# Three passes of a fused kernel hand their weights, halves and first rows on to the pass ahead

## The chip, the cores and the metric

The kernel runs on one core of a Trainium2 chip. The metric is device time in microseconds (us); three runs of the kernel before gave 2746.31, 2747.47 and 2748.63, the median is 2747.47. The profile is of one execution, with a span of 2744.8 us from the first to the last instruction.

## The reference

Two layers over x (8 batches of 512 rows of 512 values). Each adds a gated attention and a gated feed-forward to x, each after a layer norm:

```python
x = x + tanh(g_xattn[0]) * L0_xattn(layernorm(x), fside, fside, ctx, Wq, Wk, Wv, Wlq, Wlk, Wo, bo)
x = x + tanh(g_ffn[0])   * L0_ffn(layernorm(x), w1, conv_w, conv_b, w2)      # ternary weights, depthwise conv, silu
x = x + tanh(g_xattn[1]) * L1_xattn(layernorm(x), ctx, ctx, Wq, bq, Wk, bk, Wv, bv, Wo, bo)
x = x + tanh(g_ffn[1])   * L1_ffn(layernorm(x), wf, uf, bf, wi, ui, bi, wc, uc, bc, wo, uo, bo, in_c)
```

The first attention has 16 heads over 512 keys with a router matrix between queries and keys; the third line attends to 77 context rows. The last line is a recurrence over the 8 batches: `f, i = sigmoid(x wx + c wu + b)`, `g = tanh(...)`, `c = f * c + i * g`, and an output projection with the last state.

## The kernel before

Six passes run one after the other: context, attention, feed-forward, context attention, recurrence, output. A `Pass` has its own SBUF tiles, PSUM banks and semaphores; between two passes all engines meet at a barrier and the semaphores are cleared. Each pass writes its rows to a scratch tensor in HBM (`heads`, `x2`, `x3`, `columns`), and the next reads them.

In a pass each engine runs a hand-written list of instructions with semaphore waits, in the same order each turn; a turn is one batch of 512 rows. `clock` runs turn 0, a hardware loop over the middle turns, and the last two turns written out. Engines take their instructions in order: a wait holds all that stands behind it on that engine. SyncE issues nearly all DMAs, also in order.

A matrix product in full precision is made of three products of halves: a tile is split into a high half (ScalarE's copy to float32r) and a low half (VectorE's subtraction of the high half from the tile). `Weights` (line 120) does this for a pass's weights at its start: `load` on SyncE, `hi` on ScalarE, `lo` on VectorE, and TensorE waits for the last low half. `LayerNorm` (line 456 on) takes statistics and aggregates on VectorE (`moments`), a power on GpSimd (`pool_power`), and scales on VectorE (`scale`).

What stands at the starts:

- Feed-forward (`quantised_ffn_pass`): SyncE loads the output weights `Wo` of the attention (L133), the first heads (L1116) and first rows (L1117), then small constants, among them the convolution weights (L1124) and 16 loads of the convolution's bias `cb` (L1128). TensorE's `attention_out` (L1197 to L1202) needs the halves of the weights and of the heads and the bias row `BO` (L1348, L1462). VectorE waits for all constants, makes the diagonals (L1465, L1467), and adds the rows (`row_tile`, L1485).
- Context attention (`context_attention_pass`): SyncE loads three small constants (L1763 to L1765), the first rows, `Wq` and `Wo`, then keys and values. ScalarE first waits for the constants and takes a tanh (L1930), then makes high halves. VectorE makes low halves, then normalises the first rows. TensorE transposes them (L1863) and projects them to queries (L108).
- Recurrence (`recurrence_pass`): rows first, then eight loads in stages: three input weights `WX`, three state weights `WU` (each stage is free again once its low half is made), and the output's two at the end. TensorE transposes rows (L2176), then multiplies them with `WX` (L2186) and, after two column groups, the first state with `WU` (L2201).

What stands in the tails: in the attention, turn 7, quad 3 is the last quad of heads; ScalarE takes exponentials (L901), GpSimd sums them (L726, L730), and the sums gate the last output. In the feed-forward, the last turn has no next batch; VectorE scales hidden pairs (L1530, `scaled`), takes maxima of magnitudes (L1538, `magnitude`, then `fold`), TensorE convolves (L1243, waits for `scaled`), and after `fold` the token maxima, the quantisation and the second product of the last batch follow one after the other. In the context attention a turn has four groups; in each VectorE takes maximum and difference of the scores (L2011, L2014), ScalarE exponentials (L1959) and copies (L1954), GpSimd the probabilities (L1837) and, in the fourth group, the residual (L1842). TensorE's scores of the next group (L1887) wait for VectorE's difference of the present one.

## Time and profile before

| | us |
|---|---|
| median of three runs | 2747.47 |
| the profiled execution | 2746.55 |
| its span, first to last instruction | 2744.8 |

| engine | busy us | share of the span |
|---|---|---|
| TensorE, matmuls | 2364.8 | 86% |
| VectorE | 1412.0 | 51% |
| ScalarE | 1027.8 | 37% |
| GpSimd | 599.5 | 22% |

| pass | from | to | TensorE busy | VectorE busy | ScalarE busy |
|---|---|---|---|---|---|
| context | 0 | 115 | 73.3 | 53.5 | 41.6 |
| attention | 115 | 1063 | 838.3 | 488.4 | 414.6 |
| feed-forward | 1063 | 1636 | 478.2 | 379.6 | 269.4 |
| context attention | 1636 | 2055 | 344.4 | 287.3 | 169.9 |
| recurrence (to the first output loads) | 2055 | 2640 | 539.0 | 166.9 | 116.9 |
| output | 2640 | 2745 | 91.7 | 36.4 | 15.4 |

A row of the timeline gives the start and the length of an instruction or a merged run of the same one, its engine, line, operation, output and inputs, and the count; in brackets stands how long the engine sat idle ahead of it and what ended that. SPq is SyncE's queue of DMA issues: its length is the time of issuing, not that of the transfer. Idle time counts only where the engine is the one that others wait for.

### The profile page before, as it was taken

What the parts mean: (1) busy time and instruction counts of PE and PEld (TensorE: products, weight loads), DVE (VectorE), ACT (ScalarE), POOL (GpSimd) and SP (SyncE); (2) the same over time, 40 slices, a digit from 0 to 9 for tenths busy, and PEclk for the clock granted to TensorE, in tenths of its full rate; (3) what the DMA queues carried; (4) which work ended last, traced back from release to release, by engine and by line L of the source; (5) the groups of instructions that cost most, each with busy time, mean ns of one, the idle gap of its engine ahead of it and who ended that gap; (6) DMA issues with size and microseconds to landing.
All of it is one profiled execution on the core that took longest, in us unless ns stands there. A gap on an engine that the chain in (4) does not pass through costs nothing. (4 is left out here: it accounts for less than half of the span.)

```text
span 2744.8 us, 40758 instructions
## 1 busy us (share of the span) xinstructions
PE 2364.8 (86%) x16307; PEld 1555.8 (57%) x16348; DVE 1412.0 (51%) x1733; ACT 1027.8 (37%) x1185; POOL 599.5 (22%) x204
## 2 busy tenths in 40 slices
PE   7259999999999994789999866998977999999978
PEld 6235545555555552444454424666755788888856
DVE  5345555554555542577677646887734222222224
ACT  3324453444544542444555533444433111111211
POOL 0004554553645553000000001333220000000000
PEclk9669999999999997899999987999987999999989
DMA  7701011010110004011111011222114111111156
GB/s 237 179 33 37 15 42 44 10 45 10 45 41 14 13 9 134 33 43 51 46 55 53 17 68 66 70 82 69 68 58 164 47 46 46 46 46 46 46 230 259
DMA packets 104571, 182.56 MB, mean 67 GB/s; under 512 B 17252, under 2 KB 39780, under 8 KB 99358
## 3 DMA queue, kind: packets, MB, share of 16 engines
q1 hardware_dynamic: 100110, 172.84, 19.0%
q10 hardware_dynamic: 4368, 8.39, 0.8%
q8 instruction: 69, 1.13, 0.2%
q14 instruction: 24, 0.20, 0.0%
HBM read 122.07 MB, written 59.15 MB: 66 GB/s over the span
## 5 line engine op out<-in xcount | busy, mean ns | idle before, releaser
L973 DVE TENSOR_REDUCE att_mx<-att_sn 128x2 f32<-128x1024 f32 x256 | 313.7, 1225 | 189.9 <-PE att_sn L818 187.2
L730 POOL TENSOR_TENSOR att_es<-att_es,att_num 128x2048 f32<-128x2048 f32 x64 | 292.7, 4574 | 15.7 <-ACT att_num L901 9.4
L901 ACT ACTIVATE att_num<-att_st 128x2048 f32<-128x2048 f32 x128 | 240.4, 1878 | 131.0 <-PE att_st L806 67.0
L726 POOL TENSOR_TENSOR att_es<-att_num 128x2048 f32<-128x2048 f32 x32 | 145.8, 4558 | 395.8 <-PE att_pj L788 379.2
L2287 ACT ACTIVATE rec_ga<-rec_g,rec_bg 128x512 f32<-128x512 f32 x84 | 57.2, 689 | 311.9 <-PE rec_g L2186 311.9
L818 PE MATMUL att_sn<-att_kh,att_qh 32*128 32x512 f32 x512 | 128.7, 498 | 26.3 <-DVE att_mx L973 26.3
L1530 DVE TENSOR_TENSOR ffn_hs<-ffn_h,ffn_fb 128x1024 f32<-128x1024 f32 x64 | 78.1, 1220 | 115.9 <-PE ffn_h L1230 106.9
L1230 PE MATMUL ffn_h<-ffn_xqt,ffn_w 128*128 128x512 bf16 x486 | 118.8, 388 | 16.7 <-DVE ffn_hs L1530 13.1
L818 PEld LDWEIGHTS att_sn<-att_kh,att_qh 32*128 32x128 f32 x512 | 48.9, 188 | 146.1 <-DVE att_mx L973 100.0
L1837 POOL TENSOR_TENSOR xat_pr<-xat_e,xat_rd 128x1232 f32<-128x1232 f32 x32 | 73.1, 2284 | 244.0 <-DVE xat_rd L2023 237.2
L781 PE MATMUL att_pj<-att_num,att_v 128*32 128x512 f32 x1024 | 123.5, 602 | 1.0 <-issue 1.0
L1243 PE MATMUL ffn_c<-ffn_hs,ffn_dg 32*32 32x512 f32 x3072 | 114.2, 629 | 10.7 <-issue 4.2
L476 POOL TENSOR_TENSOR ffn_ln_rstd<-ffn_ln_var,ffn_ln_power 128x4 f32<-128x4 f32 x8 | 18.4, 2297 | 440.8 <-DVE ffn_ln_var L497 440.8
L2355 DVE SCALAR_TENSOR_TENSOR rec_ga<-rec_ga,rec_c 128x512 f32<-128x512 f32 x32 | 22.1, 690 | 171.4 <-ACT rec_ga L2287 171.4
L1382 ACT ACTIVATE ffn_ss<-ffn_c,ffn_cb 128x512 f32<-128x512 f32 x128 | 77.4, 692 | 70.7 <-PE ffn_c L1243 65.3
L476 POOL TENSOR_TENSOR rec_ln_rstd<-rec_ln_var,rec_ln_power 128x4 f32<-128x4 f32 x8 | 8.5, 1059 | 432.6 <-DVE rec_ln_var L497 432.6
L1954 ACT ACTIVATE xat_pt<-xat_pt 77x512 f32<-77x512 f32 x128 | 73.7, 588 | 77.7 <-PE xat_pt L1896 77.3
L1230 PEld LDWEIGHTS ffn_h<-ffn_xqt,ffn_w 128*128 128x128 bf16 x512 | 47.6, 100 | 86.3 <-issue 21.9
L1278 PE MATMUL ffn_a<-ffn_w,ffn_sq 128*128 128x512 bf16 x338 | 81.8, 387 | 11.0 <-ACT ffn_sq L1404 9.4
L1896 PEld LDWEIGHTS xat_pt<-xat_ident,xat_pr 128*77 128x77 f32 x512 | 62.8, 152 | 45.4 <-issue 23.3
L1896 PE MATMUL xat_pt<-xat_ident,xat_pr 128*77 128x128 f32 x512 | 78.6, 285 | 9.4 <-POOL xat_pr L1837 7.9
L1404 ACT ACTIVATE ffn_sq<-ffn_s 128x2048 bf16<-128x2048 int8 x32 | 61.3, 1916 | 66.1 <-DVE ffn_s L1565 66.1
(375 smaller groups left out, 5873.3 us busy)
## 6 DMA issues: line engine op xcount, KB each, us to landing
att_x<-in_x SPq DMA_DIRECT2D x8, 1024.0 KB, 5.5
att_f<-in_fside_BxSxS SPq DMA_DIRECT2D x8, 1024.0 KB, 7.6
heads<-att_o SPq DMA_DIRECT2D x32, 256.0 KB
ffn_ol<-heads SPq DMA_DIRECT2D x8, 1024.0 KB, 5.3
ffn_x<-in_x SPq DMA_DIRECT2D x8, 1024.0 KB, 5.5
x<-ffn_xr SPq DMA_DIRECT2D x32, 256.0 KB, 2.0
xat_x<-x SPq DMA_DIRECT2D x8, 1024.0 KB, 5.2
xat_xr<-x SPq DMA_DIRECT2D x8, 1024.0 KB
```

Source lines behind the costliest of these rows:

```text
L726: pool.tensor_tensor(ES[:], E[0][:], E[1][:], ALU.add).then_inc(s_sum, 1)
L730: pool.tensor_tensor(ES[:], ES[:], E[k][:], ALU.add).then_inc(s_sum, 1)
L781: last = pe.matmul(out[heads(j), :], V[:, k, c * P + DH * j:c * P + DH * j + DH], E[k][:, j, :], start=(k == 0), stop=(k == T - 1))
L818: last = pe.matmul(sn_ps[:, r, :], QT[0][c][own, m // 2 * P:m // 2 * P + P], KT[0][c][own, :], start=True, stop=True)
L901: act.activation(E[k][:], st_ps[:], ACT.Exp, scale=SCALE).then_inc(s_exp, 1)
L973: dve.tensor_reduce(MX[c % 2][:, m // 2, 2 * DH * (m % 2):2 * DH * (m % 2) + DH + 1:DH], sn_ps[:], AX, ALU.max, negate=True).then_inc(s_ma ...
L1230: last = pe.matmul(h_ps[:, m, :], W1[:, k, i * P:i * P + P], XQT[:, k, :], start=(k == 0), stop=(k == C - 1))
L1243: last = pe.matmul(c_ps[quarter(m), r, :], DG[quarter(r), 3 * (HG * group + m) + k, :], HS[group % 2][quarter(r), m, k:k + S], start=(k == ...
L1278: last = pe.matmul((a_ps, b_ps)[OUT_BANK[front][t]][:], SQ[:, i, t * P:t * P + P], W2[:, i, :], start=(i == 0), stop=(i == HT - 1))
L1382: act.activation(SS[:, i, :], c_ps[:, r, :], ACT.Silu, bias=CB[:, i:i + 1]).then_inc(s_silu, 1)
L1530: dve.tensor_tensor(HS[group % 2][:, 2 * half:2 * half + 2, 1:S + 1], h_ps[:], FB[:].unsqueeze(1).broadcast_to([P, 2, S]), ALU.mult).then_ ...
L1896: last = pe.transpose(pt_ps[j % 2][0:G, t * P:t * P + P], PR[d % 2][:, j, t, :], ident[:])
```

## The change

Tiles that were a pass's own become shared: `rows` and `rows_b` (rows and normalised rows), `weights_a` and `weights_b` (two pairs of halves), and three pairs `row_weights`. The weights that a pass needed at its start are loaded and split in the last turns of the pass ahead, and the first rows are loaded there too, for the context attention and the recurrence also normalised.

- Attention: SyncE, in its last turn, loads the feed-forward's `Wo`, the first rows and the first heads. Ahead of the last quad ScalarE makes two high halves (weights, heads) and VectorE two low halves (`following`).
- Feed-forward: its start has none of the three large loads and no halves. In its last turn SyncE loads `Wq` and `Wo` of the context attention; ScalarE makes both high halves after the third activation group (`next_high`), VectorE both low halves between hidden pairs 6 and 7 (`next_low`); then SyncE loads the first rows of `x2`, and VectorE normalises them ahead of the last maximum of magnitudes (`next_rows`).
- Context attention: ScalarE issues the loads of the three input weights into a new tile `STAGE` at the ends of groups (6,0), (6,2) and (7,0), and makes the high halves at the ends of (6,1), (6,3) and (7,1); VectorE makes the low halves there. SyncE loads the first rows of `x3`; VectorE takes their statistics at the end of group (7,2) and scales them at the end of (7,3), after a power on GpSimd.
- Recurrence: starts with three state weights to load; the two last output loads change places and stages.

```diff
@@ attention_pass
+            sp.wait_ge(made["x"], QUADS)
+            sp.wait_ge(made["f"], QUADS)
+            sp.dma_start(F[:], kxn(next_w)).then_inc(s_nextw, 16)
+            sp.dma_start(X[:], rows(x, 0)).then_inc(s_nextx, 16)
+            sp.wait_ge(made["k"], QUADS)
+            sp.wait_ge(s_store, C * 16)
+            sp.dma_start(f32(W_QO[1][1][:]), rows(o_s, 0)).then_inc(s_nexto, 16)
             turn(B - 1)
...
+            def following():
+
+                act.wait_ge(s_nextw, 16)
+                act.wait_ge(made["q"], QUADS)
+                act.activation(W_QO[0][0][:], F[:], ACT.Copy).then_inc(s_nexthi, 1)
+                act.wait_ge(s_nexto, 16)
+                act.wait_ge(made["k"], QUADS)
+                act.activation(W_QO[1][0][:], f32(W_QO[1][1][:]), ACT.Copy).then_inc(s_nexthi, 1)
...
+            def following():
+
+                dve.wait_ge(s_nexthi, 1)
+                dve.tensor_tensor(W_QO[0][1][:], F[:], f32(W_QO[0][0][:]), ALU.subtract).then_inc(s_nextlo, 1)
+                dve.wait_ge(s_nexthi, 2)
+                dve.tensor_tensor(W_QO[1][1][:], f32(W_QO[1][1][:]), f32(W_QO[1][0][:]),
+                                  ALU.subtract).then_inc(s_nextlo, 1)
...
@@ quantised_ffn_pass
-            w.load(sp)
-            sp.dma_start(f32(OL[:]), batch_rows(o_s, 0)).then_inc(s_o, 16)
-            sp.dma_start(X[:], batch_rows(x, 0)).then_inc(s_x, 16)
+            sp.sem_inc(s_o, 16)
+            sp.sem_inc(s_x, 16)
             sp.dma_start(undo[:], undo_s).then_inc(s_undo, 16)
...
+            sp.wait_ge(s_rows, B * ROWS_N)
+            sp.dma_start(XN[:], kxn(next_wq)).then_inc(s_nextw[0], 16)
+            sp.wait_ge(s_xm, B)
+            sp.dma_start(X[:], kxn(next_wo)).then_inc(s_nextw[1], 16)
+            sp.wait_ge(s_nextlo, 2)
+            sp.wait_ge(s_store, T * 16)
+            sp.dma_start(X[:], batch_rows(x2_s, 0)).then_inc(s_nextx, 16)
             turn(B - 1, True, False, False)
...
                 silu(b, 2)
+                if not front:
+                    next_high()
...
                 scaled(b, 6)
                 if front:
                     row_maxima(rows)
+                else:
+                    next_low()
                 scaled(b, 7)
...
                 if front:
                     scaled(b + 1, 0)
+                if not front:
+                    next_rows()
                 magnitude(b, 3)
                 fold(b)
...
@@ context_attention_pass
-            load_x(0)
-            w.load(sp)
+            sp.sem_inc(s_x, 16)
+            load_x(1)
             load_keys(0, 0)
...
+                if c == 3 and isinstance(b, int) and b == B - 1:
+                    ln.pool_power(pool, B)
...
+            def next_load(n):
+                if n:
+                    act.wait_ge(s_nextlo, n)
+                act.dma_start(STAGE[:], kxn(next_w[n])).then_inc(s_nextw, 16)
...
+            def next_low(n):
+
+                dve.wait_ge(s_nexthi, n + 1)
+                dve.tensor_tensor(NEXT[n][1][:], STAGE[:], f32(NEXT[n][0][:]), ALU.subtract).then_inc(s_nextlo, 1)
...
+                at = (b - B + 2) * C + c if isinstance(b, int) else -1
+                if 0 <= at < 6 and at % 2:
+                    next_low(at // 2)
+                if isinstance(b, int) and b == B - 1:
+                    if c == 2:
+                        dve.wait_ge(s_nextx, 16)
+                        ln.moments(dve, Steps(s_next, 0, ln.DVE_N))
+                    if c == 3:
+                        after = Steps(s_next, 0, ln.DVE_N)
+                        after.done = 2 * T + 1
+                        dve.wait_ge(made["x"], B * C)
+                        ln.scale(dve, B, after)
...
@@ recurrence_pass
-        names = [(gates[n][0], WX[n], 1.0) for n in range(3)] + \
-                [(gates[n][1], WU[n], 0.5) for n in range(3)] + [(wo, WO, 1.0), (uo, WX[0], 0.5)]
-        NW, NG = len(names), 6
-        whole_stages = [GA[:, 0:C, :], C2[:], X[:], XN[:]]
+        names = [(gates[n][1], WU[n], 0.5) for n in range(3)] + [(wo, WO, 1.0), (uo, WX[0], 0.5)]
+        NW, NG = len(names), 3
+        whole_stages = [GA[:, 0:C, :], C2[:], XN[:], SW[:]]
...
-            sp.dma_start(X[:], rows(x3_s, 0)).then_inc(s_x, 16)
+            sp.sem_inc(s_x, 16)
             load(sp, 0)
             load(sp, 1)
```

## Rows read from the trace of the kernel before

**Rows 1.** Timeline at the start of the feed-forward: start, length, engine, line, operation.

```profile
1068.59 1.91 ACT L138 ACTIVATE ffn_woh<-ffn_xn 128x2048 fp32r<-128x2048 f32 x1 [11.76 <-DMA ffn_xn<-in_L_xattn_Wo]
1070.53 2.29 DVE L143 TENSOR_TENSOR ffn_wol<-ffn_xn,ffn_woh 128x2048 fp32r<-128x2048 f32 x1 [10.88 <-ACT ffn_woh L138]
...
1076.48 0.77 PE L1197 MATMUL ffn_a<-ffn_bo,ffn_pick 128*128 128x512 f32 x1 [17.57 <-DVE ffn_bo L1462]
...
1083.60 0.39 DVE L1465 TENSOR_REDUCE ffn_diagonal<-ffn_ident 128x32 f32<-128x128 f32 x1 [7.38 <-DMA ffn_cb<-in_L_ffn_conv_b]
...
1085.70 0.74 DVE L1485 SCALAR_TENSOR_TENSOR ffn_x<-ffn_a,ffn_tgx,ffn_x 128x512 f32<-128x512 f32 x1
```

**Rows 2.** Timeline at the start of the context attention.

```profile
1640.82 0.20 ACT L1930 ACTIVATE xat_tg<-xat_tg 128x2 f32<-128x2 f32 x1 [19.97 <-DMA xat_bq<-in_L_xattn_bq]
...
1661.82 1.94 PE L1863 MATMUL xat_pj<-xat_ident,xat_xn 128*128 128x128 f32 x8 [29.51 <-DVE xat_xn L502]
...
1667.80 0.77 PE L108 MATMUL xat_pj<-xat_xth,xat_wqh 128*128 128x512 f32 x1 [1.50 <-DVE xat_xtl L2005]
```

**Rows 3.** Timeline at the start of the recurrence.

```profile
2055.65 0.09 POOL L2159 MEMSET rec_ones<- 2x2 f32 x1
...
2060.54 2.47 DVE L488 BATCH_NORM_STATS2 rec_ln_stats<-rec_x 128x6 f32<-128x512 f32 x4 [10.78 <-DMA rec_x<-x]
...
2063.72 1.02 POOL L476 TENSOR_TENSOR rec_ln_rstd<-rec_ln_var,rec_ln_power 128x4 f32<-128x4 f32 x1 [7.93 <-DVE rec_ln_var L497]
...
2066.84 1.94 PE L2176 MATMUL rec_pj<-rec_ident,rec_xn 128*128 128x128 f32 x8 [17.93 <-DVE rec_xn L502]
...
2075.19 0.79 PE L2186 MATMUL rec_g<-rec_xth,rec_wx0h 128*128 128x512 f32 x1 [1.41 <-DVE rec_xtl L2319]
```

**Rows 4.** Bias loads `cb`, by tile: count, shortest, median, longest ns; first and last start.

```profile
L1128 SPq DMA_DIRECT2D ffn_cb<-in_L_ffn_conv_b x16: 432/432/7212, 1067.6 to 1081.5; - x16
```

**Rows 5.** Timeline: a convolution of the feed-forward that follows on idle time.

```profile
1565.37 4.87 PE L1243 MATMUL ffn_c<-ffn_hs,ffn_dg 32*32 32x512 f32 x96 [2.90 <-ACT ffn_ss L1382]
```

**Rows 6.** Windows of TensorE: stretch, us, busy (x), granted clock, DMA share, GB/s.

```profile
1566.00:1567.00 1.00, 1.00 (x37) 0.50 0.08 16
```

**Rows 7.** Timeline of the feed-forward's last turn.

```profile
1588.60 1.22 DVE L1530 TENSOR_TENSOR ffn_hs<-ffn_h,ffn_fb 128x1024 f32<-128x1024 f32 x1 [3.67 <-PE ffn_h L1230]
...
1591.95 3.40 PE L1243 MATMUL ffn_c<-ffn_hs,ffn_dg 32*32 32x512 f32 x96
...
1599.79 2.29 DVE L1538 TENSOR_TENSOR ffn_am<-ffn_am,ffn_ab 128x2048 f32<-128x2048 f32 x1
```

**Rows 8.** Timeline of the attention's last quad.

```profile
1028.96 9.25 POOL L730 TENSOR_TENSOR att_es<-att_es,att_num 128x2048 f32<-128x2048 f32 x2
...
1032.28 1.88 ACT L901 ACTIVATE att_num<-att_st 128x2048 f32<-128x2048 f32 x1 [2.37 <-PE att_pj L781]
...
1040.24 4.54 POOL L726 TENSOR_TENSOR att_es<-att_num 128x2048 f32<-128x2048 f32 x1 [2.03 <-PE att_pj L788]
```

**Rows 9.** Timeline: VectorE's scaling in the context attention while GpSimd is busy.

```profile
1941.60 8.09 DVE L502 TENSOR_SCALAR xat_xn<-xat_x,xat_ln_mv,xat_ln_rstd 128x512 f32<-128x512 f32 x4
```

**Rows 10.** Timeline of the last two turns of the context attention.

```profile
1971.22 0.59 ACT L1954 ACTIVATE xat_pt<-xat_pt 77x512 f32<-77x512 f32 x1 [2.63 <-PE xat_pt L1896]
...
1977.58 1.13 PE L1887 MATMUL xat_s<-xat_k,xat_qt 32*128 32x77 f32 x32
...
1987.51 1.44 DVE L2011 TENSOR_REDUCE xat_mx<-xat_s 128x16 f32<-128x1232 f32 x1 [0.57 <-PE xat_s L1887]
...
1991.01 1.06 ACT L1954 ACTIVATE xat_pt<-xat_pt 77x512 f32<-77x512 f32 x2
...
1996.95 1.13 PE L1887 MATMUL xat_s<-xat_k,xat_qt 32*128 32x77 f32 x32
...
2027.74 4.52 POOL L1842 TENSOR_TENSOR xat_xr<-xat_xr,xat_bo 128x2048 f32<-128x2048 f32 x1
...
2034.21 0.69 DVE L2005 TENSOR_TENSOR xat_atl<-xat_pj,xat_ath 128x512 fp32r<-128x512 f32 x1 [8.76 <-ACT xat_ath L1949]
```

More of the change, by code:

```diff
@@ L638, in heads, with clock @@
             return slice(DH * j, DH * j + DH)
-        def clock(eng, step, ahead, late):
+        def clock(eng, step, ahead, late, following=None):
             ahead()
@@ L649, in clock @@
                 for i in range(C):
+                    if turn == B - 1 and i == C - 1 and following:
+                        following()
                     step(turn, i)
@@ L929, in late @@
                     job(task)
-            clock(act, step, ahead, late)
+            def following():
[5 more added lines that the diff above has]
+                act.activation(W_QO[1][0][:], f32(W_QO[1][1][:]), ACT.Copy).then_inc(s_nexthi, 1)
+            clock(act, step, ahead, late, following)
         @block.vector
@@ L1026, in late @@
                     job(task)
-            clock(dve, step, ahead, late)
+            def following():
[4 more added lines that the diff above has]
+                                  ALU.subtract).then_inc(s_nextlo, 1)
+            clock(dve, step, ahead, late, following)
 def row_broadcast(pe, out, columns, ident):
@@ L1101, in quantised_ffn_pass @@
         FIRST, LAST = 2, B - 2
+        s_nextw = [ps.sem(f"nextw{i}") for i in range(2)]
+        s_nexthi, s_nextlo, s_nextx, s_next = (ps.sem(n) for n in ("nexthi", "nextlo", "nextx", "next"))
         block = ps.block()
@@ L1181, in _ @@
             pe.wait_ge(s_ident, 11)
-            w.wait(pe)
             pe.wait_ge(s_bo2, 2)
@@ L1727, in context_attention_pass @@
         s_pt, s_pte = ps.sem("pt"), ps.sem("pte")
+        STAGE = ps.sb("stage", [P, C, D])
+        s_nextw = ps.sem("nextw")
+        s_nexthi, s_nextlo, s_nextx, s_next = (ps.sem(n) for n in ("nexthi", "nextlo", "nextx", "next"))
         block = ps.block()
@@ L1851, in _ @@
             pe.wait_ge(s_ident, 2)
-            w.wait(pe)
             def job(turn, task):
@@ L2291, in gates_and_state @@
                     state_high(act, b + 1, c)
-            for i in range(3, NG):
+            for i in range(NG):
                 high_half(act, i)
@@ L2311, in _ @@
         def _(dve):
-            first = Steps(s_dve, 0, ln.DVE_N)
-            dve.wait_ge(s_x, 16)
-            ln.rows(dve, 0, first)
+            dve.sem_inc(s_dve, ln.DVE_N)
+            dve.sem_inc(ln.s_var, 1)
             def rows_low(a):
@@ L2326, in _ @@
             dve.scalar_tensor_tensor(CC[:, :, 1], C0[:], 2.0, f32(CC[:, :, 0]), ALU.mult, ALU.subtract).then_inc(s_cc, 1)
-            for i in range(2, NG):
+            for i in range(NG):
                 low_half(dve, i)
```

132 lines of the change are left out of this document (72 added, 60 removed).

## The prediction

> **What bounds the kernel now.** I read the profile in this order: the engine shares of the page, the timeline around each start of a pass, the list of waits there, and the timeline of each pass's last turns. TensorE is busy 86% of the span, and most of what is missing lies where one pass hands over to the next. At the start of the feed-forward it waits 17.57 us for the first matmul [rows 1], at that of the context attention 29.51 us [rows 2], at that of the recurrence 17.93 us [rows 3]. Nothing else runs there: each stretch is a load, a split into halves and a normalisation, one after the other, so what shortens that chain shortens the run. The last turns, where the change puts this work, are the opposite: TensorE, ScalarE and VectorE hand tiles around with little slack, and each takes its instructions in order. So the sum is made per pass: what its start gives, less what the tail ahead of it costs.
>
> **Start of the feed-forward: -7.0.** The loads of the output weights, of the first heads and of the first rows leave SyncE's queue. The end of this start isn't the weights but the constants: VectorE waits until 1083.60 for the last of the 16 small bias loads and adds the first rows at 1085.70 [rows 1]. Of those 16, all but one issue in 0.43 us; one took 7.21 [rows 4]. That one is the first behind the three 1 MB loads, which I take to hold it. Gone, they give 7.21 - 0.43 = 6.8, and SyncE reaches the small loads some 0.8 earlier (three issues of about 0.5 less the wait for GpSimd's identity). The load of the convolution weights stays ahead of them and may hold the first for about 1. I take 7.0, bounds 6.3 and 7.6. TensorE's first products move from 1076.48 to about 1068.6, but their rows are added only at 1085.70 - 7.0, so TensorE idles for about 3 us in between. After an idle time of 2.90 us the 96 convolution matmuls took 4.87 us [rows 5] where 3.40 is usual [rows 7]: the granted clock shows 0.50, the lower level of 1.2 GHz, just behind the wait [rows 6]. So +1.5 (0 to 1.9).
>
> **Tail of the attention: +2.6.** Ahead of the last quad ScalarE makes two copies of 1.91 and VectorE two subtractions of 2.29 [rows 1]. ScalarE is free from about 1029.9, so its first exponential goes from 1032.28 to 1033.8, and the 1.5 shrinks to about 1.0 by GpSimd's first sum at 1040.24 [rows 8]. VectorE is idle there, but GpSimd runs two sums over 9.25 us [rows 8]. Does it hold VectorE? In the context attention four VectorE instructions that take 1.9 elsewhere took 8.09 beside GpSimd's [rows 9]. If the two exclude each other here, the second subtraction (after 2.29 for the first and the end of GpSimd's 1038.2) ends at about 1042.8, and the sum starts there: +2.6. With nothing held it is +1.0. I take 2.6, the nearest row, and 4 as the upper end.
>
> The Trainium skill says the same of the port (SBUF — State Buffer, SBUF: two separate sides): a VectorE instruction with two inputs in SBUF and a GpSimd instruction that reads SBUF lock each other out for a whole instruction. By it the term is 2.6 and by a free port 1.0; the row agrees, though of another instruction kind.
>
> **Start of the context attention: -22.0.** First rows come normalised and the weights split, so TensorE can transpose at once (about 1637). What is late next is the small constants: ScalarE waits for them until 1640.82 [rows 2], and its copy of the first columns stands behind. From the first transposition (1661.82) to the first projection (1667.80) it is 5.98, and the first 1.1 of it is done by then: 1641.0 + 4.9 = 1645.9, which is 21.9 earlier. Bounds 21.5 and 22.5. The next rows are loaded at once and hidden.
>
> **Tail of the feed-forward: +11.6.** VectorE takes its two low halves between its products for hidden pairs 6 and 7; the latter stands at 1588.60 [rows 7]. It waits for ScalarE, which makes the high half only after the third activation group, from about 1588.1 to 1590.0. Then two times 2.29: pair 7 starts at 1594.6, 6.0 late. TensorE's last convolution, at 1591.95, needs it: it starts at 1595.85, +3.9, and after that idle time at the low clock, +1.5 as above. The first rows of the next pass (statistics, power, scaling) stand ahead of VectorE's maximum at 1599.79 [rows 7], on which the last token maxima and with them all of the tail wait; they take 6.2 (2060.54 to 2066.84 in [rows 3]). The loads are early: weights by 1568, rows by 1601. Sum 11.6, bounds 9 and 13.
>
> **Start of the recurrence: -13.4.** GpSimd's last constant is there at 2055.74; with 5.98 for the columns, as above, the first gate matmul comes at 2061.8 instead of 2075.19 [rows 3]. The state weights are now the first that are loaded; my reckoning has the third ready at about 2082.7 and needed at 2084.7, so they are hidden by 2 us. Bounds 10 and 13.6.
>
> **Tail of the context attention: +13.3.** Three high halves stand at the ends of three groups on ScalarE, three low halves at the ends of the same groups on VectorE, which then can't begin the next group's maxima. First: ScalarE's last copy ends at 1971.8, the high half at 1973.7, the low one at 1976.0, maximum and subtraction (1.44 each) at 1978.9; TensorE's scores at 1977.58 [rows 10] wait for that, +1.4, and the exponential behind it holds further copies, +0.6. Second: VectorE was free at 1987.51, but ScalarE's copies end at 1992.1, at 1994.1 with the 2.0; so 1996.0, 1998.3, 2001.2 against scores due at 1996.95 + 2.0 [rows 10]: +2.3, and +1.6 behind it. Third, like the first: +1.8. Then the statistics of the next pass, 3.2 less the overlap (2060.54 to 2063.72 in [rows 3]), on VectorE's own chain: +3.1. At the end the scaling waits for GpSimd, busy with the residual until 2032.3 [rows 10], plus 1.02 for the power, plus 1.9: 2035.3 against 2034.21, +1.0. With one fall of TensorE's clock, +1.5, it is 13.3. Bounds: 8, if the stalls fill idle time further back, and 18, with three falls of the clock.
> The three loads issued from ScalarE's queue cost nothing that I can see: it idles after each of those groups. In steady turns nothing changes but the names of tiles. The output weights' last load comes later in the recurrence, but waits in front of 8 us of TensorE work: nothing.
>
> **The sum.** -7.0 + 1.5 + 2.6 = -2.9; -22.0 + 11.6 = -10.4; -13.4 + 13.3 = -0.1. Together -13.4: of 42.4 us of removed waiting some 29 come back in the tails. The profiled execution took 2746.55 us (span 2744.8 and 1.75 around it), 0.9 below the median: 2733.2 there, 2734 as a median. All terms at their best give -25.7 (-6.6 - 13.5 - 5.6), at their worst +2.1 (-0.4 - 8.5 + 8.0 = -0.9, and 3 for what the steady turns may shift).
>
> **Rivals.**
> *The copies are hidden.* VectorE is busy 51% and ScalarE 37%, so the tails absorb the copies; only the first rows' 6.2 and 3.1 stay. -42.4 + 1.5 + 9.3 = -31.6: 2716. For it: idle time before most instructions there; against it: both engines take instructions in order, and the idle time lies at other places than the copies. 0.12.
> *The small loads are held by something else.* If the 7.21 us [rows 4] are those of the convolution weights, many tiny pieces ahead of them, the first start gives 0.8 and no idle of TensorE: 2746.55 - 13.4 + 6.2 - 1.5, so 2739 as a median; and the change doesn't do there what it says. For it: it is the load directly ahead. Against: the three large ones were still landing. 0.15.
> *The waits of VectorE are carried whole.* If what VectorE loses by waiting for ScalarE's high halves (6.0 in the feed-forward; 4.4, 8.8 and 4.5 in the context attention) and both copies in the attention (8.4) reach the end undiminished, with 6.2, 3.1 and 1.0 and a fall of the clock, 1.5, at each of seven places, it is 42.4 against 52.9: 10.5 us slower, 2758. It decides from 42.4 us of added work on. Against it: TensorE has work queued at each place. 0.05.
> The summed forecast has 0.60, within 2726 to 2742; 0.08 is left to mixtures near no change.
>
> **Chances.** A measurement of this kernel can tell 0.2%, 5.5 us, from no change. Faster than 2742: nearly all of the forecast (0.58), the hidden case (0.12), most of the second rival (0.12): 0.83 with rounding. Within: 0.12. Slower: 0.05. The range of 8 in 10 is 2720 to 2744: it leaves out most of the hidden case and the slower one.
>
> **What would show it.** In the changed profile: VectorE's first wait in the feed-forward for a bias load ends about 1076.5 plus the 2.6; the last token maxima of the feed-forward come 11 to 12 us later relative to the pass's start plus 2.9 earlier; the first projection of the context attention stands about 9.6 us after the pass's first instruction instead of 31.6; the first gate matmul about 6.7 after, instead of 20.1; and before VectorE's low halves stand waits for ScalarE. Wrong would be: no wait of VectorE there, a bias load that still takes 7 us to issue, or a clock that falls in steady turns.

## The result and the profile after

The changed kernel takes 2740.69 us (median of 17 runs, 2739.44 to 2744.93) against 2746.31 for the kernel before beside it (17 runs, 2741.31 to 2750.17): a ratio of 0.9982, with an interval from 0.9975 to 0.9990. It is faster by 5.6 us or 0.2%, where 13.4 us (0.49%) were forecast. The profiled execution took 2740.13, with a span of 2738.3 us where before had 2744.8.

Each pass begins with an instruction of GpSimd that fills the identity, so its start can be read in both traces. That divides the 6.5 us of the spans by pass (profiled executions; the forecast is the sum of the terms that lie in the pass, the attention's tail in its own):

| stretch | before | after | change | forecast |
|---|---|---|---|---|
| up to the feed-forward | 1063.12 | 1065.55 | +2.4 | +2.6 |
| feed-forward | 573.12 | 583.22 | +10.1 | +6.1 |
| context attention | 418.82 | 413.01 | -5.8 | -8.7 |
| recurrence to the end | 689.7 | 676.5 | -13.2 | -13.4 |
| sum | 2744.8 | 2738.3 | -6.5 | -13.4 |

The inner two rows miss by 4.0 and 2.9 us. The outer two came as forecast, but the first of them says little: in ten profiles of kernels whose attention is the same, the feed-forward begins anywhere from 1062.1 to 1067.9. The attention's part is therefore read at its last quad, below.

The page of the changed kernel, engine shares (before, TensorE was busy 86% of its span):

```profile
PE 2388.5 (87%) x16348; PEld 1567.2 (57%) x16348; DVE 1416.6 (52%) x1733; ACT 1027.5 (38%) x1185; POOL 603.1 (22%) x204
```

The starts. Selected lines of the timelines of the changed kernel (start, length, engine, line, operation, in brackets the idle time ahead and what ended it), first of the feed-forward, then of the context attention, then of the recurrence; they answer to [rows 1 to 3]:

```profile
1070.14 0.76 PE L1226 MATMUL ffn_a<-ffn_bo,ffn_pick 128*128 128x512 f32 x1 [8.86 <-DVE ffn_bo L1497]
1080.13 0.37 DVE L1500 TENSOR_REDUCE ffn_diagonal<-ffn_ident 128x32 f32<-128x128 f32 x1 [10.09 <-DMA ffn_cb<-in_L_ffn_conv_b]
1082.21 0.75 DVE L1520 SCALAR_TENSOR_TENSOR rows<-ffn_a,ffn_tgx,rows 128x512 f32<-128x512 f32 x1
1083.01 0.79 PE L1226 MATMUL ffn_a<-ffn_bo,ffn_pick 128*128 128x512 f32 x1 [4.66 <-DVE rows L1520]
...
1118.69 5.07 PE L1272 MATMUL ffn_c<-ffn_hs,ffn_dg 32*32 32x512 f32 x96 [1.41 <-DVE ffn_hs L1565]
...
1653.59 0.20 ACT L1983 ACTIVATE xat_tg<-xat_tg 128x2 f32<-128x2 f32 x1 [21.09 <-DMA xat_bq<-in_L_xattn_bq]
...
1658.61 0.76 PE L108 MATMUL xat_pj<-xat_xth,weights_a_h 128*128 128x512 f32 x1 [1.50 <-DVE xat_xtl L2071]
...
2068.49 0.79 PE L2266 MATMUL rec_g<-rec_xth,row_weights_h 128*128 128x512 f32 x1 [1.41 <-DVE rec_xtl L2393]
```

The first projection of the context attention stands 9.84 us after that pass's start at 1648.77 (before: 31.6), the first gate matmul of the recurrence 6.7 after 2061.78 (before: 20.1). Both are what was forecast, to 0.3 us. In the feed-forward VectorE's wait for the bias loads ends 14.6 us after the pass's start, before it was 20.5: 5.9 us saved, of 7.0. Then TensorE waits 4.66 us ahead of its third set of products (a set is the 13 products for one group of 128 rows; a batch has four), and the first convolution takes 5.07.

The tails. Selected lines of the timelines of the changed kernel: the attention's last quad (it answers to [rows 8]), the feed-forward's last turn ([rows 7]), the context attention's last turns ([rows 10]):

```profile
1032.01 3.94 DVE L1050 TENSOR_TENSOR weights_a_l<-rows_b,weights_a_h 128x2048 fp32r<-128x2048 f32 x1 [2.59 <-ACT weights_a_h L945]
1035.88 6.63 DVE L1052 TENSOR_TENSOR weights_b_l<-weights_b_l,weights_b_h 128x2048 fp32r<-128x2048 f32 x1
1040.51 1.94 PE L798 MATMUL att_pj<-att_es,att_ones 128*32 128x512 f32 x8 [0.52 <-POOL att_es L740]
1042.61 4.53 POOL L736 TENSOR_TENSOR att_es<-att_num 128x2048 f32<-128x2048 f32 x1 [2.25 <-PE att_pj L798]
...
1590.16 2.29 DVE L1614 TENSOR_TENSOR weights_a_l<-rows_b,weights_a_h 128x2048 fp32r<-128x2048 f32 x1 [4.95 <-ACT weights_a_h L1448]
1594.57 1.22 DVE L1565 TENSOR_TENSOR ffn_hs<-ffn_h,ffn_fb 128x1024 f32<-128x1024 f32 x1
1610.98 2.29 DVE L1573 TENSOR_TENSOR ffn_am<-ffn_am,ffn_ab 128x2048 f32<-128x2048 f32 x1
1616.31 1.08 PE L1282 MATMUL ffn_a<-ffn_ident,ffn_am 128*128 128x128 f32 x4 [8.62 <-DVE ffn_xr L1608]
...
1985.68 2.86 DVE L2105 TENSOR_TENSOR row_weights_l<-xat_stage,row_weights_h 128x2048 fp32r<-128x2048 f32 x1 [7.23 <-ACT row_weights_h L2016]
1991.51 1.13 PE L1940 MATMUL xat_s<-xat_k,xat_qt 32*128 32x77 f32 x32 [2.70 <-DVE xat_sm L2080]
2038.31 1.92 DVE L502 TENSOR_SCALAR rows_b<-rows,xat_ln_mv,xat_ln_rstd 128x512 f32<-128x512 f32 x4 [7.88 <-POOL xat_ln_rstd L476]
```

VectorE waits for ScalarE's high halves, as forecast: 4.95 us in the feed-forward and 7.23 at the middle group of the context attention (2.04 and 2.05 at the others). The steady turns have no new wait.

A single execution can't weigh 3 us in this kernel. Where two kernels do the same, matching instructions drift apart and come back, as TensorE's clock falls in one execution and not in the other. A second profile of the changed kernel, taken with a later set of runs, has the last convolution of the feed-forward's steady turns 515.2 us after the pass's start, the first profile 511.5; yet both passes come out alike, at 584.7 and 583.2, and the context attention at 413.2 and 413.0. So I compare within a pass and, across kernels, the ratios of many runs to the kernel before that ran beside them, whose own median lay between 2744.8 and 2748.4 in the five sets of runs.

### The profile page after: what moved, and what is told of

Read it like the earlier page. It is cut to its first block and busy times, and to the rows that moved or that the text cites. A ratio compares the mean times of both kernels' runs of the same rounds, so it can differ in the third digit from the quotient of the medians.

```text
span 2738.3 us, 40819 instructions
## 1 busy us (share of the span) xinstructions
PE 2388.5 (87%) x16348; PEld 1567.2 (57%) x16348; DVE 1416.6 (52%) x1733; ACT 1027.5 (38%) x1185; POOL 603.1 (22%) x204
## 5 line engine op out<-in xcount | busy, mean ns | idle before, releaser
L2266 PE MATMUL rec_g<-rec_xth,row_weights_h 128*128 128x512 f32 x384 | 153.7, 400 | 10.9 <-ACT rec_ga L2362 9.5
L2266 PE MATMUL rec_g<-rec_xtl,row_weights_h 128*128 128x512 f32 x384 | 152.4, 397 | 0.0
L2266 PE MATMUL rec_g<-rec_xth,row_weights_l 128*128 128x512 f32 x384 | 152.0, 396 | 0.0
```

Of the source, the lines that this page charges most:

```text
L2266: last = pe.matmul(g_ps[m % 2][n][:], W[n][a][:, k, m * P:m * P + P], R[c][:, k, :], start=(part == 0 and k == 0 and i == 0), stop=((part ...
```

## Experiments

**One part undone.** If the forecast's balance of the parts is right, undoing the part at the feed-forward's start costs 2.9 us, and undoing that at the recurrence's start 0.1. The edit of the first: no loads and halves in the attention's tail, and in the feed-forward

```diff
-            sp.sem_inc(s_o, 16)
-            sp.sem_inc(s_x, 16)
+            w.load(sp)
+            sp.dma_start(f32(OL[:]), batch_rows(o_s, 0)).then_inc(s_o, 16)
+            sp.dma_start(X[:], batch_rows(x, 0)).then_inc(s_x, 16)
```

> The changed kernel without its part at the feed-forward's start: the attention loads and splits nothing ahead, the feed-forward loads its output weights, first heads and first rows itself as before; the two other parts stay. By the forecast this part was worth 2.9 us, so without it the changed kernel's 2740.7 becomes 2743.6. By my reading of the two traces the part is worth nothing (the attention's tail pays 2.1, the start gains 5.9, and TensorE at the low clock gives 4 of that back): 2740.4, and in the trace the convolution behind the first hidden pairs takes 3.4 us again instead of 5.1.

Measured: 2741.4 us (12 runs), 0.9975 of before (0.9964 to 0.9987). The whole changed kernel, in another set of runs, gave 2741.58 (7 runs) and 0.9971 (0.9960 to 0.9982):

> The changed kernel as it is, beside the others on this chip. It was 0.9982 of the kernel before. Theory: 0.998 again, with single executions spread over some 5 us because TensorE's clock falls at different places in each. If the experiments' gains were a matter of the chip, it comes out near 0.996.

So the part at the feed-forward's start brings nothing that can be measured. In the trace of the kernel without it the first convolution takes 3.40 us again, as expected. The pass takes 585.6 in place of 583.2 and 584.7, and the passes ahead of it end 2.0 us earlier, which is within their scatter.

The second, with the recurrence as before and no next loads, halves or first rows in the context attention:

> The changed kernel without its part at the recurrence's start: the context attention's last two turns carry no loads, halves or statistics of the recurrence, which starts as before. By the forecast this part was worth 0.1 us: 2740.8. By my reading of the two traces the tail pays 16.6 us for a start that is 13.3 shorter, so the kernel gets faster without it: 2737.4 (2736 to 2739). A rival, that the later passes gain elsewhere from the part: above 2741.

Measured: 2737.38 (8 runs), 0.9960 (0.9947 to 0.9973). Against the 7 runs of the whole changed kernel on the same chip it is 4.2 us less, and its slowest run (2738.91) is below their fastest (2739.84); by the ratios it is 3 to 6 us. The context attention takes 396.8 us in place of 413.0, the rest 678.4 in place of 666.0 to its last VectorE instruction. The tail costs 16.2 us for a start that is 12.4 shorter: this part loses time.

**The context attention's tail, work moved and not shortened.** In VectorE's groups

```diff
                 minus_max(b, c)
+                at = (b - B + 2) * C + c - 1 if isinstance(b, int) else -1
+                if 0 <= at < 6 and at % 2:
+                    next_low(at // 2)
...
-                if 0 <= at < 6 and at % 2:
-                    next_low(at // 2)
...
-                    if c == 2:
+                    if c == 3:
                         ln.moments(dve, Steps(s_next, 0, ln.DVE_N))
```

and the scaling goes to `late`, ahead of the first output rows.

> The changed kernel with VectorE's work in the context attention's tail moved, not shortened: each low half stands behind the next group's maximum and subtraction instead of ahead of them, the statistics of the recurrence's first rows behind the last sums, their scaling behind the last low halves of the heads. The theory that the tail pays for VectorE's waits for ScalarE's high halves (2.0, 7.2 and 2.1 us ahead of the low halves) and for the clock that falls behind them: the tail's 16.6 us go down to 3 to 6, 2729 (2727 to 2732). The rival that the added instructions themselves (3 copies of 1.9, 3 subtractions of 2.3, statistics and scaling 5.1) cost what they last wherever they stand: 2739 to 2742. A third, that only the 2.0 + 7.2 + 2.1 go: 2733 to 2735 with the clock falling as before.

Measured: 2728.38 (6 runs), 0.9932 (0.9915 to 0.9949): 11 to 14 us less than the changed kernel by the ratios, with the same instructions. The pass takes 400.2 us, so of the tail's 16.2 only 3.4 are left. VectorE still waits for the middle high half, but behind the maximum (timeline of this kernel):

```profile
1979.34 1.44 DVE L2077 TENSOR_REDUCE xat_mx<-xat_s 128x16 f32<-128x1232 f32 x1 [0.56 <-PE xat_s L1940]
1985.75 4.13 DVE L2105 TENSOR_TENSOR row_weights_l<-xat_stage,row_weights_h 128x2048 fp32r<-128x2048 f32 x1 [3.50 <-ACT row_weights_h L2016]
```

The low half even takes 4.13 us here, beside an addition of GpSimd. It was not the length of the work that cost, but that the maximum stood behind it.

With the low halves alone moved:

> The changed kernel with only the three low halves in the context attention's tail moved behind the next group's maximum; the statistics and the scaling of the recurrence's first rows stay ahead of the last maximum and of the last halves. By the trace, low halves with their waits and the low clock behind them cost some 12 of the tail's 16.6 and the rows 3 to 4. Theory: two thirds or more of the gain of both moves (11 to 13 us) is here: ratio to before 0.9948 (0.994 to 0.996), 2732. Rival, the rows' 4 us and their fall of the clock are the main part: 0.997 to 0.998.

Measured: 2732.75 (6 runs), 0.9936 (0.9923 to 0.9948); the pass takes 406.2. So 6.8 us of the pass come from the low halves and 6.1 from the first rows' statistics and scaling. My two thirds for the low halves do not hold in the trace, where it is about half; in the medians (8.8 of 13.2) they do, but the ratios of these two kernels lie within each other's intervals. The forecast had 4.1 for the rows; that the low clock behind them makes up the rest is likely, but wasn't tried by itself.

**The clock in that tail.** Behind the middle group the granted clock falls. Windows (stretch, us, busy time of each engine, clock, DMA) of the kernel before and of the changed one:

```profile
1992.00:2007.00 15.00, 14.05 (x135) 10.48 (x136) 8.39 (x9) 7.86 (x13) 6.28 (x3) 1.00 0.04 13
```

```profile
1992.00:2007.00 15.00, 14.15 (x97) 10.10 (x93) 7.04 (x8) 5.63 (x9) 4.50 (x2) 0.54 0.25 82
```

The changed one makes 97 matmuls in the time of 135, at 1.2 GHz for nearly all of it (2.4 GHz is the level shown as 1.00). To price that by itself, TensorE got work that nobody reads in the wait ahead of the late scores:

```diff
+                    if j == 1 and c == 0 and last:
+                        pe.wait_ge(s_pte, (B - 2) * H + HG * 3 + 1)
+                        for n in range(11):
+                            pe.matmul(pt_ps[0][:], W["q"][0][:, 0, 0:P], W["q"][0][:, 1, :], start=True, stop=True)
```

> The changed kernel with 11 products that nobody reads on TensorE in the context attention's last turn, ahead of the scores that wait 2.7 us for VectorE's late maximum. Theory: in this wait, and the one before it, the clock falls to its lower level for some 14 us (1992 to 2007), which costs 3.5 of the tail's 16.6. Filled, the transpositions behind the scores take 0.14 each in place of 0.29 and the passage behind them is 3 to 4 us shorter: ratio to before 0.9965 (the changed kernel has 0.998 and 0.997), 2737. Rival, the fall comes from the waits ahead of this one, or falls later all the same: no change, 0.9977.

The window of this kernel:

```profile
1992.00:2007.00 15.00, 13.20 (x126) 10.10 (x120) 8.33 (x10) 7.53 (x12) 4.50 (x2) 1.00 0.25 82
```

The clock is at 1.00 throughout, and from the late maximum to the first output row behind it the kernel takes 4.7 us less than the changed one. But in this execution the maximum came 1.6 us later (its low half took 4.5 beside GpSimd), and 3.1 remained, of a pass of 409.9 in place of 413.0. The median, 2739.51 (10 runs), and the ratio, 0.9976 (0.9965 to 0.9987), can't tell this from no change.

Did the filler hold the clock up? The second profile of the changed kernel, which has no filler, leaves that open. Its timeline and windows at the first group and at the middle one:

```profile
1971.83 1.13 PE L1940 MATMUL xat_s<-xat_k,xat_qt 32*128 32x77 f32 x32 [1.27 <-DVE xat_sm L2080]
1974.41 1.99 PE L1949 MATMUL xat_pt<-xat_ident,xat_pr 128*77 128x128 f32 x8
...
1997.78 1.13 PE L1940 MATMUL xat_s<-xat_k,xat_qt 32*128 32x77 f32 x32 [2.15 <-DVE xat_sm L2080]
```

```profile
1973.00:1983.00 10.00, 9.27 (x36) 5.22 (x36) 6.93 (x8) 4.52 (x7) 2.25 (x1) 0.52 0.82 271
1998.00:2008.00 10.00, 8.20 (x100) 5.98 (x97) 6.94 (x8) 5.82 (x9) 2.97 (x2) 1.00 0.34 122
```

Here the clock falls one group earlier, behind a wait of 1.27 us, behind which the first profile has it at 1.00; at the middle group, behind 2.15 us, it stays up. From the late maximum to the first output row it is 13.6 us, the same as with the filler, against 18.3 in the first profile. The early fall costs 4.3 us at its own place, and the whole pass is as long as before. So the price of one fall in this tail is shown by the traces, 4.3 and 4.7 us. That the filler prevents it is not shown, nor what it is worth over many runs.

**The clock at the feed-forward's start.** The same with 18 products ahead of the third set and 12 ahead of the second hidden pair:

```diff
             for t in range(T):
+                if t == 2:
+                    for n in range(18):
+                        pe.matmul(c_ps[:, n % HG, :], pick[:], BO[:], start=True, stop=True)
                 attention_out(0, t)
```

> The changed kernel with products that nobody reads on TensorE, 18 ahead of the third set of the feed-forward's first output products, where it waits 4.7 us, and 12 ahead of the second pair of hidden tiles, where it waits 3.8 us; they go to banks that are written anew later, and the output stays what it was. Theory: these waits make the clock fall to its lower level and that costs 2.3 us in the third set and 1.7 in the first convolution. Filled, the clock stays at 1.0, the third row addition comes 2.3 us earlier, the convolution takes 3.4 again: 2737 (2736 to 2739). Rival, the clock falls whether TensorE works or not, or the filler's own time costs as much: 2740 to 2743.

Measured: 2734.92 (6 runs), 0.9963 (0.9949 to 0.9977), against 0.9982 and 0.9971 for the changed kernel: by the ratios 5 or 2 us less, on a chip where the kernel before, too, was faster (2744.81). Timeline of this kernel, to be held against 1118.69 and its 5.07 us above:

```profile
1112.11 3.40 PE L1272 MATMUL ffn_c<-ffn_hs,ffn_dg 32*32 32x512 f32 x96 [1.41 <-DVE ffn_hs L1571]
```

Windows of the third set, in the changed kernel and in this one:

```profile
1083.00:1088.00 5.00, 4.99 (x12) 3.92 (x13) 2.03 (x3) 0.00 (x0) 0.00 (x0) 0.50 1.04 442
```

```profile
1080.00:1085.00 5.00, 4.49 (x20) 3.73 (x21) 3.67 (x6) 0.00 (x0) 0.00 (x0) 1.00 0.99 426
```

Counted from the first row addition, the third gains 2.4 us on the changed kernel, the second hidden pair 1.7, the convolution 1.7: 5.8 in all. Since the small loads end 0.9 later in this execution, 4.8 of them are left against the pass's start, and over the whole pass 3.3 (580.0 in place of 583.2; 584.7 in the second profile). The fall at this place is no accident of one execution: the first convolution takes 5.07 and 5.14 in the two profiles of the changed kernel. Added work makes this stretch shorter, so what these waits cost there was the clock.

**What the start waits for.** The gate loads get a semaphore of their own, and the diagonals are made behind the first quantised rows:

```diff
-            sp.dma_start(TGX[:], gx.partition_broadcast(P)).then_inc(s_const, 16)
+            sp.dma_start(TGX[:], gx.partition_broadcast(P)).then_inc(s_gates, 16)
...
-            act.wait_ge(s_const, 304)
+            act.wait_ge(s_gates, 32)
```

> The changed kernel with the two small gate loads on a semaphore of their own and the diagonals for the convolution made behind the first quantised rows, so that the feed-forward's first row addition no longer waits for the 16 small bias loads. Theory: those loads are what the start waits for, and the pause of TensorE behind them brings the low clock. The first addition then comes at about 1075.5 in place of 1082.2, TensorE makes its four sets in one go, and the first hidden pairs come 7 to 9 us earlier: 2733 (2731 to 2735). Rival, the diagonals or the weights loaded behind become the wait: 2737 to 2741.

Measured: 2732.4 (6 runs), 0.9951 (0.9937 to 0.9965). Timeline and window of this kernel:

```profile
1076.45 0.75 DVE L1516 SCALAR_TENSOR_TENSOR rows<-ffn_a,ffn_tgx,rows 128x512 f32<-128x512 f32 x1 [5.90 <-PE ffn_a L1231]
```

```profile
1076.00:1080.00 4.00, 4.00 (x20) 3.28 (x19) 2.16 (x3) 0.00 (x0) 0.00 (x0) 1.00 0.18 5
```

The first addition waits for TensorE, no longer for a load; TensorE works without a pause at the full clock, and behind the first convolution 8.9 us are gained, counted from the pass's start. The pass takes 574.2 in place of 583.2. The semaphore and the later diagonals were changed together; what each gives by itself wasn't tried.

**What holds the small loads.** In the kernel before, the load of the convolution weights was put behind the 16 small ones:

```diff
-            sp.dma_start(CW[:].rearrange("p (i k) -> p i k", k=3),
-                         conv_w.rearrange("(i p) o k -> p i (o k)", p=P)).then_inc(s_const, 16)
             for group in range(GROUPS):
...
+            sp.dma_start(CW[:].rearrange("p (i k) -> p i k", k=3),
+                         conv_w.rearrange("(i p) o k -> p i (o k)", p=P)).then_inc(s_const, 16)
```

> The kernel before, with the load of the convolution weights issued behind the 16 small bias loads and no longer ahead of them. My prediction put the 7.2 us that the first small load took to issue down to the three 1 MB loads. If so, it still takes 6 to 7 us. The rival is that the convolution weights ahead of it hold it: then all 16 take 0.4 each. In the changed kernel, without the three large loads, one still took 2.3, so between: 4.5 to 5.5 (the large loads' share alone).

The small loads by tile (count; shortest, median and longest ns), in the changed kernel and in this one, which answer to [rows 4]:

```profile
L1151 SPq DMA_DIRECT2D ffn_cb<-in_L_ffn_conv_b x16: 431/432/2329, 1069.0 to 1078.0; - x16
```

```profile
L1126 SPq DMA_DIRECT2D ffn_cb<-in_L_ffn_conv_b x16: 432/434/1073, 1066.7 to 1074.8; - x16
```

With the three large loads and without the convolution weights ahead of it, the longest took 1.07; without the large loads and with the weights, 2.33; with both, 7.21. Neither alone makes the 7.2: it is the weights' load that holds the next one, and for longer while three large ones are in flight. Of a gain of 4.7 us at VectorE's wait, though, counted from the pass's start, nothing is left behind the first convolution: the convolution takes 5.14 us at the low clock in that kernel too, and its one time, 2749.42, is no better than before.

**The attention's tail.** VectorE's low halves go behind GpSimd's last sum:

```diff
             def late():
+                dve.wait_ge(s_sum, QUADS * 3)
+                dve.wait_ge(s_nexthi, 1)
+                dve.tensor_tensor(W_QO[0][1][:], F[:], f32(W_QO[0][0][:]), ALU.subtract).then_inc(s_nextlo, 1)
                 for task in LATE:
                     job(task)
```

and the second one behind the loop.

> The changed kernel with the attention's two low halves on VectorE moved behind GpSimd's last sum: one there, where VectorE waits for TensorE's last transpositions, one behind the last output rows. Theory, that VectorE's subtractions and GpSimd's sums hold each other (3.9 and 6.6 us in place of 2.3, the pair of sums 11.1 in place of 9.2): both low halves take 2.3, the sums 9.2, and the attention ends 1.9 to 2.1 earlier: 2738.7. Rival, that ScalarE's two copies ahead of the last quad cost it: 2740 to 2741 and the last quad's sum starts as late as before.

Measured: 2739.43 (12 runs), 0.9979 (0.9969 to 0.9990), where the changed kernel had 0.9982 and 0.9971: no gain that can be told from none. GpSimd's pair of sums is back at its length (timeline of this kernel), but the next sum waits longer:

```profile
1026.34 9.27 POOL L740 TENSOR_TENSOR att_es<-att_es,att_num 128x2048 f32<-128x2048 f32 x2
1039.14 4.53 POOL L736 TENSOR_TENSOR att_es<-att_num 128x2048 f32<-128x2048 f32 x1 [3.53 <-PE att_pj L798]
```

From the pair to the next sum it is 12.8 us; 13.4 in the changed kernel and 11.3 before [rows 8]. So the two engines do hold each other, for 1.9 us of GpSimd's time, but only 0.6 of that reaches the end; the other 1.5 are ScalarE's copies, which delay TensorE's column sums, and the clock, which is at 0.55 from 1037 to 1042.

**The feed-forward's tail.** ScalarE's high halves go behind its third magnitude, VectorE's low halves behind its maximum and behind the last token maxima, the first rows behind the last rounding:

```diff
                 magnitude(b, 2)
+                if not front:
+                    next_low(0)
...
             token_maxima(B - 1)
+            next_low(1)
             for group in range(GROUPS):
                 rounded(B - 1, group)
+            next_rows(0)
+            out_rows(B - 1, 0, False)
+            next_rows(1)
```

> The changed kernel with the work in the feed-forward's tail moved: ScalarE's two high halves behind its third magnitude, VectorE's first low half behind its maximum for it, the second behind the last token maxima, the next pass's first statistics behind the last rounding and their scaling behind the first output row. By the reading that the tail's 12.2 us are VectorE's wait, two subtractions and the first rows ahead of the convolution and of the last maximum: the tail costs 1 to 3, 2730.5 (2729 to 2733). The rival that the work costs its length wherever it stands, or that the next pass's start now waits for it: 2738 to 2742.

Measured: 2739.67 (12 runs), 0.9968 (0.9958 to 0.9979): 1 to 2 us, where 10 were expected. The trace shows the gain, 10.9 us up to the last token maxima, and then a wait that my own edit had made. Timelines of VectorE, ScalarE and SyncE in this kernel:

```profile
1623.31 4.49 DVE L1600 TENSOR_TENSOR ffn_s<-ffn_ss,ffn_qb 128x2048 int8<-128x2048 f32 x2 [7.39 <-ACT ffn_sq L1431]
...
1619.57 1.91 ACT L1488 ACTIVATE ffn_xr<-ffn_xm 128x2048 f32<-128x2048 f32 x1 [8.17 <-DMA x<-ffn_xr]
...
1610.85 0.37 SPq L1185 DMA_DIRECT2D rows<-x  x1
1611.26 24.18 SPq L1162 DMA_DIRECT2D x<-ffn_xr  x6
```

SyncE waits for the second low half ahead of the next rows' load, and its stores of batch 6 stand behind that wait. ScalarE can't overwrite the output rows until those are stored, and VectorE waits for ScalarE. With the load behind the stores:

```diff
-            sp.wait_ge(s_nextlo, 2)
-            sp.wait_ge(s_store, T * 16)
-            sp.dma_start(X[:], batch_rows(x2_s, 0)).then_inc(s_nextx, 16)
             turn(B - 1, True, False, False)
+            sp.wait_ge(s_nextlo, 2)
+            sp.wait_ge(s_store, T * 16)
+            sp.dma_start(X[:], batch_rows(x2_s, 0)).then_inc(s_nextx, 16)
```

> As the run with the feed-forward's work moved later, but SyncE issues the load of the next pass's first rows (and waits for the second low half ahead of it) behind its stores of batch 6 and no longer ahead of them. If those stores, held behind that wait, made ScalarE's copy for the last output rows 7.4 us late, that wait is gone, the tail costs 1 to 2 us in place of 12.2, and the time is 2730.5 (2728 to 2733). The rival, that the last tail is bound elsewhere (the later statistics, or the rows landing late): 2735 to 2740.

Measured: 2727.64 (6 runs), 0.9933 (0.9920 to 0.9946), and the pass takes 568.7 in place of 583.2. From pair 7 (1586.75) to the last output row (1630.48) it is 43.7 us, as in the kernel before (1588.60 to 1632.35): the work costs this tail nothing any more. Of the 14.5 us of the pass 12.2 are the tail's; the other 2.3 are there before it begins, drift as told above. The next pass takes 415.1 in place of 413.0 in this profile and gives 2.1 of them back.

**All moves together.**

> All four moves together (the attention's low halves behind GpSimd's last sum, the gate loads on their own semaphore, the feed-forward's tail and the context attention's tail with their work moved later and SyncE's load behind its stores). If each gain is its own, at its own place, they add up: against before the ratios give 0.9982 less 0.0050, 0.0049, 0.0031 and 0.0003, 0.985, so 2705 (2702 to 2709). Rival, that the gains overlap or that a pass that starts earlier waits for a load again: 2711 to 2720.

Measured: 2706.98 (5 runs, 2703.54 to 2711.0), a ratio of 0.9842 (0.9830 to 0.9855). The gains are each their own and add up, to 41 us less than before (2748.25 beside it). In the profile, which is of the slowest of the five runs, the feed-forward takes 564.9 us and the context attention 402.7, where the separate gains make 562 and 400. The changed kernel, with the same work at other places, gave 5.6. Its page:

```profile
PE 2372.0 (88%) x16307; PEld 1562.0 (58%) x16348; DVE 1417.5 (52%) x1733; ACT 1027.5 (38%) x1185; POOL 601.2 (22%) x204
```

## Why the prediction was wrong in size, step by step

The sign was right, and 13.4 us of gain were forecast where 5.6 came in the medians and 6.5 in the profiles. The sum per pass held as a method: its terms as measured add up to -6.9, where the spans differ by -6.5 (0.3 of the rest is drift ahead of the attention's last quad). The step that failed is the clock. The forecast had one fall of TensorE's clock at the feed-forward's start and one in the context attention's tail, each at +1.5, the price of one slow convolution [rows 5]. The start had two, for 3.8 together, and one fall in the tail costs 4.3 to 4.7, with a further one at its end. These two terms were too good by 3.4 and 3.3 us, and that is the miss.

**Start of the feed-forward, -5.5 forecast, -2.1 measured** (about -1.2 in the second profile). Two steps failed. The 7.21 us were put down to the three large loads; the rival said the convolution weights. The runs put both in the right only together, and without the large loads 2.33 stayed: 5.9 in place of 7.0. The larger error was in the clock. I foresaw that TensorE would idle 3 us behind its first products and took 1.5 for one fall. It idled 4.66, the third set then ran at 1.2 GHz (+2.3), and so did the first convolution (+1.9 with what hangs on it); 0.4 came back later. So 5.9 less 3.8 is 2.1. With the waits filled, third set and convolution took their full-speed times again.

**Tail of the attention, +2.6 forecast, +2.1 measured.** The size was near, but by luck: the path was another. The two engines do hold each other, and the second subtraction ended at 1042.51, with 0.27 us of drift ahead of it, where 1042.8 was worked out. The next sum, though, did not wait for it but for TensorE's column sums (1040.51 and 1.94 long, in the lines above), which waited for GpSimd's pair of sums and ran at the lower clock. The run with the low halves moved shows that nearly all of the delay would be there without the holding: what I had set at 1.0 for the copies is 1.5, through TensorE's slower column sums.

The Trainium skill (SBUF — State Buffer, SBUF: two separate sides) says that a VectorE instruction with two inputs in SBUF and a GpSimd instruction that reads SBUF lock each other out for a whole instruction. The trace agrees: 3.94 us is about the rest of GpSimd's first sum (some 1.7) and 2.29 of its own, 6.63 about a second sum (4.5) and 2.29. In the second profile the first subtraction begins earlier into GpSimd's sum, at 1029.94, and takes 5.92.

**Start of the context attention, -22.0; measured -22.4** (-21.0 in the second profile). Right, with the reason given: ScalarE's wait for the small constants ends last.

**Tail of the feed-forward, +11.6; measured +12.2.** Right, step by step: pair 7 is 5.7 late (6.0), TensorE's convolution 3.7 (3.9), its low clock 1.4 (1.5), the first rows 5.8 (6.2). Not foreseen is another fall of the clock in the 8.62 us ahead of the last token maxima, which adds 0.5 and then 0.8 at the first output row.

**Start of the recurrence, -13.4; measured -13.3.** Right.

**Tail of the context attention, +13.3; measured 16.6** (15.4 in the second profile). The steps at the first group (1.3 for 2.0), the third (1.3 for 1.8), the statistics (3.0 for 3.1) and the scaling (1.0 for 1.0) hold. The middle group has 9.2 (the scores 3.1 late, the first output row behind them another 6.1), where 3.9 was forecast for the wait and what follows. In the second profile, where the clock stays up there, it is 3.6: the wait was sized rightly. What failed is the +1.5 for one fall of the clock. In the first profile the clock stayed low for some 14 us at the middle group, in the second for some 10 at the first group (5.7 in place of 1.3), not for the 3 us of one convolution, from which I had taken the price [rows 5]. The last 0.8 is a further fall at the end.

**The rivals.** That the copies are hidden (2716) was wrong for this placement and would have been right for another: moved, the feed-forward's are hidden wholly, and in the context attention all but 3.4 us. The rival of the small loads held by something else was half right, as told. Waits carried whole (2758) did not come.

**The chances.** The measured 0.18% lies at the edge of the 0.2% that the cases were parted by; faster than that had 0.83, no change 0.12. The range up to 2744 holds the time. What was too sure was the clock: each fall was taken as 1.5 us and only some of them were counted, and those behind the first row additions and in the context attention's tail make most of the way from 2734 to 2741.

## What to carry over

When the next stage's preparation is put into a tail, look for each instruction at what stands behind it on its own engine and put it behind the one that others wait for: the same instructions cost the feed-forward's tail 12 us ahead of what TensorE waited for and nothing behind it, and the same holds for the queue that issues a load behind a wait. In a sum of stalls, give the stretch behind new pauses of TensorE a fall of the clock, with the length of the work that follows it, not a fixed price; at which pause it falls can differ from one execution to the next, so read more than one profile before a fall is put down to one wait. And before a start is shortened, ask what is late next, for a gain that ends in a pause of TensorE may be handed back within the next 40 us.

## What the runs showed of the hardware

- TensorE's clock fell to 1.2 GHz behind a wait of 4.66 us that followed on 8 us of products, and stayed there for the next 5 us. With 18 products that nobody reads in that wait it was 1.00, 2.4 GHz, behind it.
- The length of the last wait alone does not tell where the clock falls. In the context attention it fell behind a wait of 2.70 in one execution and stayed low for some 14 us, though TensorE was busy for 14.15 of the 15 us shown; in another execution of the same kernel it fell behind 1.27 and not behind 2.15.
- A load of many small pieces held SyncE's next issue: 2.33 us alone, 7.21 with three loads of 1 MB in flight, 1.07 with these and without it.
- VectorE's subtraction of 2.29 us took 3.94 and 6.63 (5.92 and 6.62 in the second profile) beside GpSimd's sums, and GpSimd's pair of sums 11.14 in place of 9.25.
- Two executions of one kernel differ by up to 14 us (the kernel before, 2741.91 to 2755.79 over 25 runs on one chip); two profiles of the changed kernel show the clock's falls at different places.
